# Attention stage: softmax sums inverted by logarithm, exponential and a Newton step; two small products moved to an idle PSUM bank

## The reference, cut to what matters

```python
x = x + xattn(layernorm(x), ctx, ctx)        # softmax(Q K^T / sqrt(32)) V, then Wo
def xattn(query, key, value):
    scores = einsum('bhqd,bhkd->bhqk', Q, K) / sqrt(Hd)
    attn = softmax(scores, axis=-1)          # the change is in how exp(...) / sum is formed
    out = einsum('bhqk,bhkd->bhqd', attn, V)
    return out.transpose(0, 2, 1, 3).reshape(B, S, D) @ Wo.T + bo
x = x + moe(layernorm(x))                    # top 2 of 8 experts, gate/up/down projections
```

## Time and profile before

| | before |
|---|---|
| median of 3 runs | 1720.36 us |
| the profiled execution | 1732.28 us |
| span of its trace | 1730.5 us |
| PE busy | 1597.8 us, 92% of the span |
| DVE busy | 1272.5 us, 74% |
| POOL busy | 837.5 us, 48% |
| ACT busy | 658.1 us, 38% |
| mean granted TensorE clock | 0.97 |

### The profile page before, as it was taken

The page is one execution under the profiler, slowest core; times in us unless marked ns, Lnnn a source line. Parts: engine busy times, 40 slices in busy tenths (PEclk is TensorE's granted clock), DMA queues, the critical chain, the costliest instruction groups (busy, mean ns, idle before and its releaser), DMA issues. The chain is left out here.

```text
span 1730.5 us, 30244 instructions
## 1 busy us (share of the span) xinstructions
PE 1597.8 (92%) x9612; PEld 1168.4 (68%) x9612; DVE 1272.5 (74%) x2414; ACT 658.1 (38%) x1267; POOL 837.5 (48%) x634
## 2 busy tenths in 40 slices
PE   6889999999899999999998469999999999999995
PEld 4445555555555555555553259999999998999994
DVE  5575777878668778687685668778888778777873
ACT  3354544535445445354444133223323234222320
POOL 3364656566566676566678321423333333423232
PEclk9999999999999999999999769999999999999997
DMA  6342333443434433424331161324543253324321
GB/s 221 84 121 66 106 112 85 112 104 88 121 80 111 103 94 94 116 75 110 92 99 33 56 223 50 101 85 166 172 147 123 87 204 121 107 85 149 116 86 61
DMA packets 101125, 188.99 MB, mean 109 GB/s; under 512 B 28192, under 2 KB 29600, under 8 KB 100960
## 3 DMA queue, kind: packets, MB, share of 16 engines
q1 hardware_dynamic: 79936, 124.25, 25.4%
q0 software_dynamic: 20832, 62.49, 11.4%
q10 hardware_dynamic: 192, 0.26, 0.0%
HBM read 204.32 MB, written 37.51 MB: 140 GB/s over the span
## 5 line engine op out<-in xcount | busy, mean ns | idle before, releaser
L802 DVE TENSOR_REDUCE negmax<-max_ps 128x2 f32<-128x1024 f32 x252 | 307.4, 1220 | 175.5 <-PE max_ps L542 174.1
L671 ACT ACTIVATE pt<-work 128x512 f32<-128x512 f32 x512 | 278.6, 595 | 263.5 <-PE work L554 256.7
L983 POOL TENSOR_TENSOR acc<-acc,pt 128x1024 f32<-128x1024 f32 x128 | 303.8, 2377 | 134.1 <-ACT pt L671 134.1
L1486 PE MATMUL gu_ps<-xgT_hi,wg_hi 128*128 128x256 f32 x1248 | 349.3, 280 | 2.3 <-DVE xgT_lo L1601 1.5
L1486 PE MATMUL gu_ps<-xgT_lo,wg_hi 128*128 128x256 f32 x1248 | 345.8, 277 | 0.0
L1486 PE MATMUL gu_ps<-xgT_hi,wg_lo 128*128 128x256 f32 x1248 | 345.5, 277 | 0.0
L980 POOL TENSOR_TENSOR acc<-pt 128x1024 f32<-128x1024 f32 x64 | 153.3, 2396 | 200.2 <-PE work L574 132.0
L1486 PEld LDWEIGHTS gu_ps<-xgT_hi,wg_hi 128*128 128x128 f32 x1248 | 235.2, 188 | 3.0 <-issue 1.9
L1747 POOL DMA_INDIRECT out<-acc,token_of x78 | 77.2, 989 | 330.4 <-DVE acc L1645 324.6
L1486 PEld LDWEIGHTS gu_ps<-xgT_lo,wg_hi 128*128 128x128 f32 x1248 | 235.5, 189 | 0.1
L1486 PEld LDWEIGHTS gu_ps<-xgT_hi,wg_lo 128*128 128x128 f32 x1248 | 235.2, 188 | 0.0
(11 more groups left out here) (221 smaller groups left out, 2902.2 us busy)
## 6 DMA issues: line engine op xcount, KB each, us to landing
raw_g<-w_gate_up SPq DMA_DIRECT2D x39, 2048.0 KB
raw_d<-w_down SPq DMA_DIRECT2D x39, 1024.0 KB
qs<-q_hi SPq DMA_DIRECT2D x252, 64.0 KB
ks<-k_hi SPq DMA_DIRECT2D x252, 64.0 KB
bd<-b_down SPq DMA_DIRECT2D x39, 256.0 KB
x_in<-x SPq DMA_DIRECT2D x36, 256.0 KB, 3.3
ctxT_raw<-ctx_t SPq DMA_DIRECT2D x32, 256.0 KB, 4.1
xln_dram<-x SPq DMA_DIRECT2D x32, 256.0 KB, 2.8
```

Of the source, the lines that this page charges most:

```text
L671: e.activation(pt[k % 2][:, h, :], in_work("exp", u, k, h)[:, :], ACT.Exp, scale=scale).then_inc(exped.sem, 1)
L802: e.tensor_reduce(negmax[:, u % 2, n:n + 2], pair_of(u, r)[:, :, :], AX.X, ALU.max, negate=True).then_inc(maxed.sem, 1)
L983: e.tensor_tensor(acc[:, heads, :], acc[:, heads, :], pt[k % 2][:, heads, :], ALU.add).then_inc(added.sem, 1)
L1486: ins = e.matmul(gu_ps[n % GU_BANKS][:, part, :], wg[s][pw][:, k, cols], xgT[s][px][:, k, :], start=(k == 0 and m == 0), stop=(k == KD - 1 ...
```

## The change

**Inverse.** The matrix of ones becomes minus one, so that the sums come out negative. ACT forms ln(-sum) from the work bank and exp of its negative, both into inv, instead of the copy (guess_inverse). DVE then makes one Newton step over all 512 columns in round 3 (refine): the product of bank and inv goes back to the bank, and (product + 2) times inv to inv. The bank of the sums is freed by refine and no longer by the copy. The four reciprocals and four products of rounds 4 to 7 become one product of 512 columns in round 5. The last unit keeps its reciprocals. ACT's table set is loaded at the stage's start by name.

**Banks.** The transposed maxima go to the o_ps bank of the unit's own parity, which idles then, and the sum of the logits to the second quarter of an o_ps bank, for tokens up to the last units. Both leave the ring, which changes which bank each other use gets. turn_max waits for the product of two units before, the logits' sum for the low part of the maxima, and weigh_values for the logits' bias addition.

**Order.** The logits' sum and its bias addition move from rounds 0 and 1 to rounds 1 and 2, the two parts of best_experts from rounds 1 and 2 to rounds 2 and 3.

```diff
             if s - 6 in tokens[:-T]:
-                at(0, ("logit_sum", s - 6))
-                at(1, ("logit_out", s - 6))
+                first = 1 if s in units else 0
+                at(first, ("logit_sum", s - 6))
+                at(first + 1, ("logit_out", s - 6))
...
-            for r, lag, *keys in ((1, 9, ("best", 0)), (2, 9, ("best", 1)), (3, 9, ("count",)), (5, 9, ("soft",)),
+            for r, lag, *keys in ((2, 9, ("best", 0)), (3, 9, ("best", 1)), (3, 9, ("count",)), (5, 9, ("soft",)),
...
             if s - 1 in units[:-1]:
-                for t in range(T):
-                    at(4 + t, ("norm", s - 1, t))
+                at(3, ("refine", s - 1))
+                at(5, ("norm", s - 1, ALL))
...
+        idle.update({("turn_max", u): o_ps[u % 2] for u in units})
+        idle.update({("logit_sum", n): o_pair[:, n % 2, P:2 * P] for n in tokens if n + 6 in units})
...
-            elif kind == "turn_max":
-                over = m_lo_made, what[0]
...
             elif kind == "sum":
-                over = copied, what[0]
                 if what[0] == units[-1]:
                     over, end = (inverted, (units[-1], T - 1)), ("norm", units[-1], T - 1)
+                else:
+                    over, end = (refined, what[0]), ("refine", what[0])
...
             def sum_logits(n):
                 to = take("logit_sum", n)
+                if n + 6 in units:
+                    e.wait_ge(m_lo_made.sem, m_lo_made[n + 6])
...
             def turn_max(u):
                 to = take("turn_max", u)
+                if u >= 2:
+                    e.wait_ge(divided.sem, divided[u - 2, ALL])
...
                     if u >= 2:
-                        e.wait_ge(divided.sem, divided[u - 2, T - 1])
+                        e.wait_ge(divided.sem, divided[u - 2, ALL])
+                    if u >= 6:
+                        e.wait_ge(logits_out.sem, logits_out[u - 6])
...
-            def copy_sums(u):
+            def guess_inverse(u):
                 e.wait_ge(summed.sem, summed[u])
...
-                e.activation(inv[:, :], in_work("sum", u)[:, :], ACT.Identity).then_inc(copied.sem, 1)
+                e.activation(inv[:, :], in_work("sum", u)[:, :], ACT.Ln, scale=-1.0).then_inc(logged.sem, 1)
+                e.wait_ge(logged.sem, logged[u])
+                e.activation(inv[:, :], inv[:, :], ACT.Exp, scale=-1.0).then_inc(guessed.sem, 1)
...
+            e.preload_act_table_set("natural_log_exp_and_others")
...
+            def refine(u):
+                to = in_work("sum", u)
+                e.wait_ge(guessed.sem, guessed[u])
+                e.tensor_tensor(to[:, :], to[:, :], inv[:, :], ALU.mult).then_inc(residue_made.sem, 1)
+                e.wait_ge(residue_made.sem, residue_made[u])
+                e.scalar_tensor_tensor(out=inv[:, :], in0=to[:, :], scalar=2.0, in1=inv[:, :],
+                                       op0=ALU.add, op1=ALU.mult).then_inc(refined.sem, 1)
+
             def normalise(u, t):
...
                 if u < units[-1]:
-                    e.wait_ge(copied.sem, copied[u])
-                    sums = inv[:, :]
...
+                    e.wait_ge(weighed.sem, weighed[u, T - 1])
+                    if c == 0 and b >= 2:
+                        e.wait_ge(out_made.sem, out_made[(b - 1) * T - 1])
+                    e.wait_ge(refined.sem, refined[u])
+                    e.tensor_tensor(oT[b % 2][:, c, :], o_ps[u % 2][:, :], inv[:, :], ALU.mult).then_inc(divided.sem, 1)
+                    return
```

More of the change, by code:

```diff
@@ L368, in attention_stage @@
         exped = Mark(sem("exped"), [(u, k, h) for u, k in TILES for h in range(GROUP)])
-        copied = Mark(sem("copied"), units)
+        logged, guessed = Mark(sem("logged"), units[:-1]), Mark(sem("guessed"), units[:-1])
         xlnT_made = Mark(sem("xlnT_made"), tokens)
@@ L384, in attention_stage @@
         m_lo_made = Mark(sem("m_lo_made"), units)
-        inverted = Mark(sem("inverted"), [(u, t) for u in units for t in range(T)])
-        divided = Mark(sem("divided"), [(u, t) for u in units for t in range(T)])
+        inverted = Mark(sem("inverted"), [(units[-1], t) for t in range(T)])
+        residue_made, refined = Mark(sem("residue_made"), units[:-1]), Mark(sem("refined"), units[:-1])
+        divided = Mark(sem("divided"), [*[(u, ALL) for u in units[:-1]], *[(units[-1], t) for t in range(T)]])
         x2_made = Mark(sem("x2_made"), tokens)
@@ L396, in attention_stage @@
         added = Mark(sem("added"), [(u, k, p) for u in units for k in range(1, T) for p in range(2)])
+        idle = {("turn_x", 0, t): bank for t, bank in enumerate((max_ps[:, 0, :], max_ps[:, 1, :], o_ps[0], o_ps[1]))}
+        idle.update({("out", tokens[-T] + j, 0): max_ps[:, j, :] for j in range(2)})
+        idle.update({("turn_max", u): o_ps[u % 2] for u in units})
+        idle.update({("logit_sum", n): o_pair[:, n % 2, P:2 * P] for n in tokens if n + 6 in units})
         at = {key: n for n, key in enumerate(ORDER)}
@@ L423, in attention_stage @@
                 over = parts_made, what[0]
-            elif kind == "logit_sum":
+            elif kind == "logit_sum" and key not in idle:
                 over, end = (logits_out, what[0]), ("logit_out", what[0])
@@ L433, in attention_stage @@
         ring = Ring(uses)
-        idle = {("turn_x", 0, t): bank for t, bank in enumerate((max_ps[:, 0, :], max_ps[:, 1, :], o_ps[0], o_ps[1]))}
-        idle.update({("out", tokens[-T] + j, 0): max_ps[:, j, :] for j in range(2)})
         in_work = lambda *key: idle[key] if key in idle else work[ring.bank[key]][:, :]
@@ L700, in on_act @@
                 elif kind == "sum" and what[0] < units[-1]:
-                    copy_sums(*what)
+                    guess_inverse(*what)
                 elif kind == "turn_max":
@@ L922, in on_dve @@
                     v_out(*what)
+                elif kind == "refine":
+                    refine(*what)
                 elif kind == "norm":
```

21 lines of the change are left out of this document (10 added, 11 removed).

## The result

The changed kernel takes 1775.95 us, the median of four runs (1770.04 to 1780.94); the kernel before took 1722.09 in the same comparison (1716.99 to 1723.84). The ratio is 1.0316, 95% interval 1.0275 to 1.0358. Forecast were 1740 and a range up to 1766: slower was right, and the loss is 54 us instead of 20. The profiled execution took 1780.94, its span is 1778.8 against 1730.5, a difference of 48.3. Of these, 47.4 have arisen when step 31 begins (974.13 after, 926.78 before). DVE is busy for 1202.9 us, 69.6 less; PE for 1617.3, 19.5 more; ACT for 676.3; POOL for 837.0. The mean clock is 0.957.

A forecast was written before the change was run, and what follows sets the result against it. A plain step was taken as bound by PE, with DVE loaded but not the bound. Losses of 3.2 + 0 + 8.4 + 8.4 = 20.0 us on the median 1720.4 gave 1740; 8-in-10 range 1714 to 1766.

The forecast's parts named there:

- c = 1, six steps with a choice of experts: DVE operation held by POOL's first addition delays counts and Newton step; PE waits 2.4 at v; 1.4 us a step, 8.4.
- the wait at k: Round 0: PE's 0.33 us wait at k for a bank with a running exponential, forecast to go.
- the bank is free late, and v waits: In c = 1, the sums' bank is free at 428.1 instead of 423.7; PE reaches v at 425.71 and stands 2.4 us.
- Rival A: In c = 1 a count is also held by POOL's second addition, PE stands 5 us, clock halves; 7.3 a step; chance 0.20.
- a fall of the clock in c = 1 steps: One of the signs that would show the forecast wrong; no size given.
- c = 2: Seven steps: exponential matmul of round 4 waits 0.7, q_lo and reduce come behind the Newton step; 1.2 a step, 8.4 us.
- SP's late issue: In c = 2, SP issues q_lo 1.8 us later; a step costs 1.8 instead of 1.0 where SP has no slack.
- c = 0 and c = 3: PE's v matmul starts 0.2 us later, waiting for the Newton step; 16 steps including two c = 1 steps, 3.2 us.
- The chain: Logarithm, exponential, product, Newton step and handoffs free the sums' bank 2.8 us after C, the start of ACT's copy; before, 0.60.
- round 0: Wait at k goes, but PE then waits for m_lo; set at 0, bounds -0.33 and +0.25 a step over 22 steps.
- DVE's relief: DVE does 2.85 us less a unit, 88 us in all, worth only what PE waits for DVE; no shorter steps.

The follow-up runs named there:

- best_alone: The kernel before with only the two parts of best_experts moved to rounds 2 and 3; 1737.25 us, ratio 1.0053.
- banks_alone: The kernel before with the new banks and order, keeping ACT's copy and the reciprocals, without the Newton step; 1751.79 us, ratio 1.0143.
- q_first: The changed kernel with q_lo ahead of the Newton step in c = 2 steps; 1771.26 us, ratio 1.0270.
- newton_alone: The changed kernel with the banks and order of the kernel before, keeping logarithm, exponential and Newton step; 1742.69 us, ratio 1.0093.
- late_ln2: The changed kernel with DVE's second layer norm scaling moved from round 3 to round 4 in c = 1 steps; 1758.12 us, ratio 1.0191.

## Why the prediction was wrong

**The step that failed** is "c = 1, six steps with a choice of experts", priced at 1.4 a step, 8.4 in all. It measured 32.5. Its mechanism (one of the five operations caught, the rest behind it, v late) was right as far as it went; it let the last count end at 426.7 and POOL's second addition start at 426.84, and took the 0.14 us between them as enough. Counted from the step's start, with the forecast's numbers first: the caught operation ends at 15.4 (measured 15.1); what follows it takes 1.1 (1.53, since pick and hot stood behind the catch as well, 0.22 each); so the counts would have ended at 16.4 (16.6); the second addition starts at 16.57 (16.28). The margin of +0.14 was -0.32.

Two things were wrong in it. The 1.1 us of work behind the catch supposes that the last of the five, hot, is the one caught; it was ranks, two operations earlier (in step 9, three). And POOL was left at its old time, when both its additions came 0.29 us earlier in the step (the first at 12.65, before at 12.94). The order brought this, and not the wait at k: best_alone keeps its wait of 0.33 at k, and its two additions start at 12.63 and 16.27. In before, the first part of best_experts stands ahead of DVE's reduce of round 2, and PE's score matmuls of round 3 start 0.05 us after that reduce ends (419.99); in best_alone that part stands behind the reduce, and the score matmuls follow q at 424.95 with no wait. The reduce in before (its step begins at 410.27), then the reduce and POOL's first addition in best_alone (415.85):

```profile
418.72 1.22 DVE L802 TENSOR_REDUCE negmax<-max_ps 128x2 f32<-128x1024 f32 x1
```

```profile
423.37 1.23 DVE L802 TENSOR_REDUCE negmax<-max_ps 128x2 f32<-128x1024 f32 x1 [0.74 <-PE max_ps L542]
...
428.49 2.37 POOL L980 TENSOR_TENSOR acc<-pt 128x1024 f32<-128x1024 f32 x1 [2.58 <-PE work L574]
```

From the step's start the reduce comes at 8.45 and at 7.52. The term "the bank is free late, and v waits" was not what made the price either: banks_alone has no Newton step, and the same two catches cost its c = 1 steps as much (35.93 for 36.06), by way of the reduce of round 4.

**Rival A** is what happened, in all six steps: waits of 4.7 to 4.9 (forecast 5), then half clock. That its time, 1740 + 6 x 5.9 = 1775, is the measured one within 1 us is in part chance: a step lost 5.4, not 7.3, which is 11 us less in all, and step 30 made up for most of that. I priced it at 1762 and gave it 0.20 on the ground that 0.1 us is less than I can work out. That ground speaks for a half, not for a fifth, and the steps are nearly alike (all six were caught twice in after, two of six in best_alone), so the range should have reached 1775. The prediction named a fall of the clock in c = 1 steps as a sign of being wrong, and it came in all six.

**The last steps were left out.** Step 30 costs 8.1, and nothing in the sum stood for it; about half is the early half clock, which no run ties to an edit. The trace of before had it: 22.29 us, 18.73 of PE, and four waits for a reduce of 0.5 to 0.86.

**c = 2** came out: 1.28 for 1.2 a step, by the two parts forecast (0.54 at the exponential matmul, 0.57 from q_lo's place). In this there is some luck. The 1.2 was a mean with a price of 0.8 for SP's late issue in it, and that it costs anything is not shown: q_first moved it back, and the next steps were no shorter. And the 9.8 for 8.4 in all hold a step of 2.57 and one of 0.07.

**c = 0 and c = 3** were forecast at 0.2 and cost 0.35 to 0.41 in c = 0; the c = 3 steps came out 6.2 us shorter in all, by stalls at their start that the change has no part in as far as is known. The chain is as forecast, C + 2.77. The rest, 0.1 to 0.2, belongs to round 0, set at nothing with a bound of +0.25: banks_alone, which has the new round 0 and no Newton step, takes 0.13 more than before, newton_alone 0.25.

**DVE's relief** was 69.6 us for a forecast 88. The 2.87 us a unit came (31 x 2.87 = 89); the held fourth counts took back 6 x 2.0 = 12, and the remaining 7 are not taken apart. As forecast, no step became shorter by it.

## What to carry to other kernels

Where two engines lock each other out, read the distance between their starts in every round that an edit touches, on both engines, and treat a distance below the error of your working as an even chance. An operation caught once pushes the next ones into the following lock, so a catch is priced at one lock and at two. Moving the operations that can be caught, or a little work ahead of them, can be worth many times its length: 0.54 us moved gave 4 us a step.

## What the runs showed of the hardware

The catch of a DVE operation with two SBUF inputs is decided within less than 0.1 us: in after's step at 422.20, L878 starts 0.04 us behind POOL's first addition and takes 2.37, and the third count starts 0.04 us ahead of the second addition and takes its 0.16. The size of the operation plays no part; a 128x8 bf16 count (0.16 us) was held for 2.2. This is the rule that the prediction names from the Trainium skill (SBUF — State Buffer, section "SBUF: two separate sides"), and these rows agree with it.

In after, each of the six waits of PE of 4.7 to 4.9 us brought half clock (1.2 GHz), for 3.4 or 6.8 us, beginning between 1.9 us into the wait and 0.1 us after its end. Waits of 2.7 to 3.3 a little later in the step (banks_alone) did the same in all six steps. Of six waits of 2.2 to 2.4 (late_ln2) three did, and so did two of 1.83 (newton_alone, steps 9 and 29). Half of the half clock that lies behind the wait, 1.7 to 2.9 us in after, is an estimate of what it adds to the wait, and a reader who prices the wait by its length alone misses that.
